# A gated attention and mixture-of-experts kernel: the routing between its halves rebuilt on other engines and types, bias loads issued from batch step eight on

## The reference

```python
x = x + tanh(g_xattn) * xattn(layernorm(x), ctx, ctx)      # retention with a decay mask
xf = layernorm(x).reshape(-1, 256)                          # 2048 tokens
scores = softmax(xf @ Wg.T)                                 # 8 experts
expert_weights, expert_indices = top_k(scores, 2)
expert_weights = expert_weights / expert_weights.sum(-1, keepdims=True)
gates = (one_hot(expert_indices, E) * expert_weights[..., None]).sum(axis=1)
h1 = xf @ (W1 + B1 A1).T + b1 ; h3 = xf @ (W3 + B3 A3).T + b3     # per expert, HID 512, rank 16
y_e = (silu(h1) * h3) @ (W2 + B2 A2).T + b2
out = x + tanh(g_ffn) * sum_e gates[e] * y_e
```

## Time and profile before

| | us |
|---|---|
| median of 3 runs | 347.4 (344.05 to 348.44) |
| profiled execution | 345.2 |
| its span, first to last instruction | 343.4 |
| busy in the span: TensorE / VectorE / ScalarE / GpSimd | 308.8 / 259.2 / 183.2 / 194.2 |
| mean granted TensorE clock | 0.968 |
| batch steps, from the start to the last top-eight search | 119.1 |
| routing, to the first matmul of the first tile | 23.2 |
| tiles, from there to the end | 201.0 |

### The profile page before, as it was taken

How to read it: one execution, slowest core, us unless ns; L and a number is a source line. 1 busy time by engine, 2 the same in 40 slices (tenths; PEclk the granted TensorE clock), 3 DMA queues, 4 the chain that set the end, 5 groups by cost and what they waited for, 6 DMA issues and landing times.

```text
span 343.4 us, 6837 instructions
## 1 busy us (share of the span) xinstructions
PE 308.8 (90%) x1766; PEld 234.3 (68%) x1766; DVE 259.2 (76%) x638; ACT 183.2 (53%) x387; POOL 194.2 (57%) x171
## 2 busy tenths in 40 slices
PE   8589989999997377999999999999999999999970
PEld 3468777778886324467777777777777777777750
DVE  2679797879996599278877788778877788777850
ACT  4646655666775611265565555655565555655540
POOL 1459886878988616514564556554564556454331
PEclk9899999899999769999999999999999999999997
DMA  7937799899878269403332233333331333234100
...
DMA packets 28098, 43.82 MB, mean 128 GB/s; under 512 B 6960, under 2 KB 15536, under 8 KB 27792
## 3 DMA queue, kind: packets, MB, share of 16 engines
...
...
## 4 chain that ended last, share of the span: by engine, by line
PE 63%; POOL 9%; DVE 8%; DMA 8%; issue 4%; ACT 4%; SPq 1%; POOLq 1%; ACTq 0%; DVEq 0%
PE bank L497 31%; PE bank L514 15%; POOL WL L700 5%; DMA xs<-x_in 5%; PE bank L505 5%; PE bank L487 2%; PE bank L345 2%; DMA WH<-lora_in 2%; DVE stage L783 2%; ACT WH L578 2%; PE bank L443 1%; PE bank L388 1%; PE bank L450 1%; DVE st L798 1%; PE bank L404 1%
## 5 line engine op out<-in xcount | busy, mean ns | idle before, releaser
L761 POOL DMA_INDIRECT out<-ys,sidx x39 | 61.9, 1586 | 85.6 <-DVE gsel L1010 61.8
L700 POOL TENSOR_TENSOR WL<-stage,WH 128x512 bf16<-128x512 f32 x48 | 60.4, 1279 | 18.1 <-ACT WH L578 17.8
L497 PE MATMUL bank<-WH,xh 128*128 x156 | 56.0, 440 | 0.6 <-ACT xh L658 0.6
L685 ACT ACTIVATE ys<-BB,gsel 128x256 f32 x39 | 19.8, 509 | 55.0 <-DMA out<-ys,sidx 52.9
L497 PE MATMUL bank<-WH,xl 128*128 x156 | 48.9, 394 | 0.0
L751 POOL DMA_INDIRECT xg<-xn_rows,gidx x39 | 38.8, 995 | 15.2 <-issue 12.4
L497 PE MATMUL bank<-WL,xb 128*128 x156 | 47.3, 385 | 0.0
L578 ACT ACTIVATE WH<-stage 128x512 fp32r<-128x512 f32 x48 | 29.6, 631 | 22.4 <-DVE stage L783 22.2
L1025 DVE TENSOR_TENSOR h<-bank,BB 128x512 f32<-128x512 f32 x39 | 27.0, 691 | 15.7 <-PE bank L497 15.6
L664 ACT ACTIVATE gh<-bank 128x512 fp32r<-128x512 f32 x39 | 23.4, 599 | 26.8 <-PE bank L505 26.8
L497 PEld LDWEIGHTS bank<-WH,xl 128*128 128x128 f32 x156 | 29.2, 188 | 7.7 <-DVE xl L1016 0.5
...
## 6 DMA issues: line engine op xcount, KB each, us to landing
...
```

Source lines behind the costliest of these rows:

```text
L497: last = nc.tensor.matmul(dst[:, :], lhs[p][:, c * P:(c + 1) * P], W[:, bass.ds(e * (UNITS * UC) + (2 * kind + c) * UC, HID)], start=(part ...
L700: nc.gpsimd.tensor_tensor(w_dst(WL, s, m), stage[(u * UNITS + m) % NSTAGE][:], w_dst(WH, s, m).bitcast(F32), ALU.subtract).then_inc(s_wl, 1)
L761: nc.gpsimd.indirect_dma_start(out=out_rows, out_offset=bass.IndirectOffsetOnAxis(ap=sidx[:, i:i + 1], axis=0), in_=ys[p][:], in_offset=No ...
```

## The change

The routing's tiles are bf16 and laid out with the 8 columns of a round innermost, so that each instruction's operands run with unit step; `AT` becomes `AT` (two buffers, two planes), `PP` and `IN2`. The scan runs over each partition's own `H` ahead of TensorE (`HS`), and TensorE's `trim` and `ones` products add up to the whole rank in one bank. GpSimd's multiplication goes to VectorE (`high`). The row number is no longer split in two sums: both parts are added by TensorE in the same columns of PSUM (two matmuls for each column of pairs, 16 a round instead of 8, whose weights are `BS[:, :, w]`), and which of the two experts it is is told by an indicator of 1 or 2 (`twice`). `gidx` is copied from PSUM at once and the gathers start on it (`s_rows`), ahead of `sidx`, `eid` and the selectors. The sums for the first 14 columns (`early_counts`) and constants (`constants`, `grids`) are made in steps 8 and 9. The wait for all stores now stands in `early_counts` and `grids`, ahead of the last top-eight search and of the last `first_two`. The search reads PSUM. The gates are multiplied and stored by ScalarE. `cst` is loaded in SP's turn 3. The bias loads wait for what last used the bytes that they overwrite; the buffers are laid out anew for it (that part of the diff, declarations only, is left out). Numbers of `keep_clock` change.

```diff
     for t in range(2, B):
         turn(t, t % 2)
+        if t == 3:
+            sp.dma_start(cst[:], consts).then_inc(s_cst, 16)
     turn(B, 0, more=False)
     turn(B + 1, 1, more=False)
-    sp.dma_start(cst[:], consts).then_inc(s_cst, 16)
-    sp.wait_ge(s_store, 32 * B)
-    sp.wait_ge(s_wl, E * UNITS)
-    sp.wait_ge(s_L, B)
+    sp.wait_ge(s_vproj, B)
+    sp.wait_ge(s_qrot, B)
+    sp.wait_ge(s_x2, B - 1)
     for e in range(E):
+        if e == 4:
+            sp.wait_ge(s_out, B)
+        if e == 6:
+            sp.wait_ge(s_unit, E * UNITS)
+        if e == 7:
+            sp.wait_ge(s_wl, (E - 1) * UNITS + 2)
         sp.dma_start(BB[:, e, :], biases[e:e + 1, :].to_broadcast([P, BCOL])).then_inc(s_bb, 16)
-        if e == 0:
-            sp.wait_ge(s_gates, 1)
-            sp.dma_start(xn2_d[:, D:D + K].rearrange("(j p) k -> p j k", p=P), gate[:]).then_inc(s_gates_d, 16)
...
         if three:
+            if not two:
+                keep_clock(10, WL, pK)
             pe.wait_ge(s_xn2, s - 1)
...
-            pos_wait(pe, s_L, s - 2)
+            pos_wait(pe, s_top, 2 * (s - 2))
...
-    Hf = H[:].rearrange("p e j -> p (e j)")
+    Hf, Cf = [t[:].rearrange("p e j -> p (e j)") for t in (H, HS)]
     pe.wait_ge(s_H, 1)
-    nc.tensor.matmul(pK[:, 0:P], tri[:], Hf, start=True, stop=True)
-    nc.tensor.matmul(pQ[:, 0:P], ones[:], Hf, start=True, stop=True).then_inc(s_rank, 1)
-    keep_clock(16, WL)
-    q = KJ // 4
-    for kj in range(KJ):
-        if kj % q == 0:
-            pe.wait_ge(s_bs, kj // q + 1)
-            pe.wait_ge(s_atj, kj // q + 1)
-            pe.wait_ge(s_atp, kj // q + 1)
-        last = nc.tensor.matmul(pV[:, 0:3 * NT_SLOTS], BS[kj // q % 2][:, kj % q, :],
-                                AT[:, kj].rearrange("p a i -> p (a i)"), start=(kj == 0), stop=(kj == KJ - 1))
-        if kj % q == q - 1:
-            last.then_inc(s_slots, 1)
-            keep_clock(4, WL)
-    keep_clock(22, WL)
+    nc.tensor.matmul(pO[:, 0:E], ones[:], HS[:, :, NJ - 1], start=True, stop=True).then_inc(s_total, 1)
+    nc.tensor.matmul(pK[:, 0:P], trim[:], Hf, start=True, stop=False)
+    nc.tensor.matmul(pK[:, 0:P], ones[:], Cf, start=False, stop=True).then_inc(s_rank, 1)
+    keep_clock(11, WL)
+    for c in range(4):
+        pe.wait_ge(s_bs, c + 1)
+        pe.wait_ge(s_hi, c + 1)
+        pe.wait_ge(s_pp, c + 1)
+        if c >= 2:
+            pe.wait_ge(s_twice, c - 1)
+        for w in range(KQ):
+            nc.tensor.matmul(pV[:, 0:2 * NT_SLOTS].rearrange("p (a i) -> p a i", a=2), BS[c % 2][:, :, w],
+                             AT[c % 2][:, :, :, w], start=(c == 0 and w == 0), stop=False)
+            last = nc.tensor.matmul(pV[:, 0:NT_SLOTS], BS[c % 2][:, :, w], PP[c % 2][:, :, w],
+                                    start=False, stop=(c == 3 and w == KQ - 1))
+        last.then_inc(s_slots, 1)
+    keep_clock(15, WL)
...
-    pe.wait_ge(s_routed, 1)
+    x_transposes(0, 0)
+    pe.wait_ge(s_eid, 1)
     read_expert(0, 0)
-    x_transposes(0, 0)
...
-        nc.scalar.activation(idxf[:, :, b * TPB:(b + 1) * TPB], I8[:, :, 0:K].rearrange("p t k -> p k t"), ACT.Copy
-                             ).then_inc(s_two, 1)
+        if b < B - 1:
+            nc.scalar.activation(idxf[:, :, b * TPB:(b + 1) * TPB], I8[:, :, 0:K].rearrange("p t k -> p k t"), ACT.Copy
+                                 ).then_inc(s_two, 1)
+    def grids():
+        act.wait_ge(s_cst, 16)
+        act.wait_ge(s_qT, 2 * B)
+        nc.scalar.activation(tiles_x[:], cst[:, C_TILE:C_TILE + NT_SLOTS].unsqueeze(2).to_broadcast([P, NT_SLOTS, KQ]),
+                             ACT.Copy).then_inc(s_grid, 1)
+        act.wait_ge(s_store, 32 * B)
+        nc.scalar.activation(slots_x[:], cst[:, C_IOTA:C_IOTA + P].unsqueeze(2).to_broadcast([P, P, KQ]), ACT.Copy
+                             ).then_inc(s_grid, 1)
...
         if two:
             hi(0, 1)
         if three:
+            if not two:
+                grids()
...
+    def planes(c):
         act.wait_ge(s_ind, c + 1)
-        nc.scalar.activation(AT[:, c * q:(c + 1) * q, 1, :], AT[:, c * q:(c + 1) * q, 2, :], ACT.Copy,
-                             scale=cst[:, C_P:C_P + 1]).then_inc(s_atp, 1)
+        if c >= 2:
+            act.wait_ge(s_slots, c - 1)
+            nc.scalar.activation(AT[c % 2][:, 1], IN2[c % 2][:], ACT.Copy, scale=2.0).then_inc(s_twice, 1)
+        nc.scalar.activation(PP[c % 2][:], AT[c % 2][:, 1] if c < 2 else IN2[c % 2][:], ACT.Copy, scale=cst[:, C_P:C_P + 1]
+                             ).then_inc(s_pp, 1)
+    planes(0)
+    act.wait_ge(s_w, 1)
+    for k, w in enumerate((wa, wb)):
+        nc.scalar.activation(gate[:, :, k], w[:], ACT.Copy, scale=tg[:, 1:2]).then_inc(s_gates, 1)
+    act.wait_ge(s_gates, K)
+    act.dma_start(xn2_d[:, D:D + K].rearrange("(j p) k -> p j k", p=P), gate[:]).then_inc(s_gates_d, 16)
+    for c in range(1, 4):
+        planes(c)
...
     act.wait_ge(s_routed, 1)
+    act.wait_ge(s_eid, 1)
+    x_parts(0, 0)
     act.wait_ge(s_bb, 16 * E)
-    x_parts(0, 0)
     tile_steps(act, tile)
...
-    pool.wait_ge(s_routed, 1)
     pool.wait_ge(s_gates_d, 16)
+    pool.wait_ge(s_rows, 1)
     for i in range(XBUF - 1):
         gather(i)
+    pool.wait_ge(s_routed, 1)
...
+    def constants():
+        dve.wait_ge(s_cst, 16)
+        dve.wait_ge(s_qT, 2 * B)
+        nc.vector.tensor_scalar(trim[:], cst[:, C_TRI:C_TRI + P], -1.0, None, ALU.add).then_inc(s_trim, 1)
+        for k in range(K):
+            nc.vector.tensor_scalar(hi_x[:, k * NJ:(k + 1) * NJ], cst[:, C_HI:C_HI + NJ], float(P), None, ALU.mult
+                                    ).then_inc(s_hix, 1)
+    def experts_of(j0, j1):
+        n = j1 - j0
+        nc.vector.tensor_tensor(OH[:, :, :, j0:j1],
+                                cst[:, C_E:C_E + E].unsqueeze(1).unsqueeze(3).to_broadcast([P, K, E, n]),
+                                idxf[:, :, j0:j1].unsqueeze(2).to_broadcast([P, K, E, n]), ALU.is_equal).then_inc(s_oh, 1)
+        dve.wait_ge(s_oh, 1 if j0 == 0 else 3)
+        nc.vector.tensor_tensor(H[:, :, j0:j1], OH[:, 0, :, j0:j1], OH[:, 1, :, j0:j1], ALU.add).then_inc(s_oh, 1)
+    def early_counts():
+        dve.wait_ge(s_two, 2 * (B - 1))
+        experts_of(0, JL)
+        dve.wait_ge(s_store, 32 * B)
+        nc.vector.memset(ones[:], 1.0)
+        nc.vector.memset(one8[:], 1.0)
...
-        def row_maxima():
+        def sorted_eight():
             dve.wait_ge(s_logit, b + 1)
-            nc.vector.tensor_copy(L8[:], pL[:, 0:TPB * E].rearrange("p (t e) -> p t e", t=TPB)).then_inc(s_L, 1)
-        def sorted_eight():
-            dve.wait_ge(s_L, b + 1)
             pos_wait(dve, s_two, 2 * b)
             for t in range(TPB):
-                last = nc.vector.max(M8[:, t, :], L8[:, t, :])
+                last = nc.vector.max(M8[:, t, :], pL[:, t * E:(t + 1) * E])
             last.then_inc(s_top, 1)
...
+        if two and not one:
+            constants()
         if two:
             dve.wait_ge(s_scores, s)
             pos_wait(dve, s_out, s - 1)
...
             if not two:
                 add(E - 1, 1, 4)
                 add(E - 1, 1, 5)
-            row_maxima()
+            if not two:
+                early_counts()
...
+    dve.wait_ge(s_top, 2 * B)
+    nc.vector.tensor_copy(idxf[:, :, JL:NJ], I8[:, :, 0:K].rearrange("p t k -> p k t")).then_inc(s_last, 1)
+    dve.wait_ge(s_last, 1)
+    experts_of(JL, NJ)
+    dve.wait_ge(s_oh, 4)
+    flat = lambda t: t[:].rearrange("p e j -> p (e j)")
+    nc.vector.tensor_tensor_scan(flat(HS), col(C_SEG, P), flat(H), 0.0, ALU.mult, ALU.add).then_inc(s_H, 1)
+    dve.wait_ge(s_two, 2 * B - 1)
+    nc.vector.tensor_tensor(dl[:], M2[:, :, 1], M2[:, :, 0], ALU.subtract).then_inc(s_dl, 1)
     dve.wait_ge(s_wl, E * UNITS)
+    dve.wait_ge(s_total, 1)
+    then(nc.vector.tensor_scalar(ti[:], pO[:, 0:E], float(P - 1), None, ALU.add))
+    then(nc.vector.tensor_scalar(ts[:], ti[:], 7, None, ALU.arith_shift_right))
+    then(nc.vector.tensor_copy(nt[:], ts[:]))
+    then(nc.vector.tensor_tensor_scan(tend[:], one8[:], nt[:], 0.0, ALU.mult, ALU.add))
+    then(nc.vector.tensor_tensor(base[:], tend[:], nt[:], ALU.subtract))
+    dve.wait_ge(s_rank, 1)
+    then(nc.vector.scalar_tensor_tensor(flat(Z), base[:].unsqueeze(2).to_broadcast([P, E, NJ]), float(P), pK[:, 0:P],
+                                        ALU.mult, ALU.add))
+    then(nc.vector.tensor_tensor(PK[:], OH[:], Z[:].unsqueeze(1).to_broadcast([P, K, E, NJ]), ALU.mult))
+    then(nc.vector.reduce_sum(pos[:], PK[:].rearrange("p k e j -> p k j e"), axis=AX))
+    then(nc.vector.tensor_copy(posi[:], pos[:].rearrange("p k j -> p (k j)")))
+    nc.vector.tensor_scalar(sli[:], posi[:], P - 1, None, ALU.bitwise_and)
+    then(nc.vector.tensor_scalar(tli[:], posi[:], 7, None, ALU.arith_shift_right))
+    nc.vector.tensor_copy(slb[:], sli[:])
+    then(nc.vector.tensor_copy(tlb[:], tli[:]))
+    dve.wait_ge(s_grid, 2)
```

(31 more changed lines are left out.)

135 lines of the change are left out of this document (39 added, 96 removed).

## The result

| kernel | median us | lowest to highest | runs |
|---|---|---|---|
| before | 347.75 | 344.05 to 348.44 | 4 |
| changed | 352.81 | 352.09 to 354.13 | 4 |

The ratio changed to before is 1.019 (95% interval 1.014 to 1.025). By the medians the change makes the kernel about 5 us slower. Forecast were 344.5 and at most 349.5: the prediction was wrong, on the sign and outside its range. The profiled execution took 352.09 us, its span is 350.2. Some executions fall in a state that is about 1% longer; the medians count them and the ratios don't, so the two differ a little in the last experiments.

The account below looks back on a forecast made before the run. Bound by the VectorE routing chain before the first tile's matmul, with tiles running gapless on TensorE: gained 6.0, lost 5 to delayed stores and 0.3 to `cst`, so 0.7 off 345.2 gives 344.5 us; range 338.5 to 349.5.

Parts of the forecast that it names:

- S: Time at which VectorE may start the last top-eight search; forecast 118.2 us if the stores are undisturbed.
- the 0.3 taken for `cst`: Moving the `cst` load into step three, where DMA is busy, costs between nothing and 0.9 us; 0.3 taken.
- I take 5 us: Delay of the last two stores, and so of the last search, by early bias loads sharing the DMA engines.
- the 5.7 from which my own text says that the sign turns: Store delay in us from which the change was forecast to make the kernel slower instead of faster.
- the first rival: Stores wait out the whole bias backlog, search starts at 127, first matmul 2.8 us later, 348.3 us; chance 17%.
- The second rival, whole turns: DMA engines alternate queues by whole turns, so stores land only 2.4 us late: 341.9 us; whole turns or less 30%.
- Top-eight to tile numbers: Routing chain from the last search's start to the tile numbers (`tlb`'s end), forecast at 5.7 us.
- The four rounds: One-hots and matmul sums of four column groups, forecast to end 7.1 + 0.5 us after the tile numbers, against 9.4 before.
- 0.5 for the stride: Extra time in the four rounds for matmul weights read at a 16-byte stride; bounds nothing and 2 us.
- To the first matmul: From summed groups to gather 0.5 us (0.2 conversion, 0.3 start), then 4.3 to the first tile's matmul.
- the third rival: Sparser routing leaves TensorE at half clock, closing dummy matmuls outlast the gather, first tile slow: 3 to 4 us, 348; 8%.
- biases cost nothing on this path: Bias loads begun ten us earlier finish before the first gather, so their own time adds nothing there.

Follow-up runs that it names:

- the kernel with two loads early: Changed kernel with bias loads 0 and 1 issued in step eight, the other six held behind the 16 stores: 345.49 us, ratio 0.998.
- The probe: Changed kernel plus 48 unused 78-column matmuls ahead of the rounds, weights and moving operand contiguous or strided: 0.063 us each with contiguous moving operand, 0.14 strided.

## Why the prediction was wrong

By its own marks: it had S at 118.2 + 5 = 123.2, t0 (`tlb`'s end) at 128.9, the gather at 137.0, the first tile matmul at 141.3. Measured were 127.59, 132.99, 143.50 and 148.34. Of the 7.0 us between, 4.4 are in S, -0.3 in the chain to t0, 2.95 behind t0. With 0.8 more in the tiles and the 0.3 taken for `cst`, which did not show up in any step before the eighth, that is the whole distance from 344.5 to the profiled 352.09.

**The step that failed: "I take 5 us" for the stores.** Measured: 9.0 more from issue to landing (12.0 for 3.0), and 0.4 from an issue at 115.52 instead of 115.15. The mechanism was right, and so was its price: one for one by packets, 32 packets of 0.2 us, 6.4; measured, the passage took 8.0 (118.6 to 126.6) instead of 1.7, 6.3 more. What the number lacked is in the two steps around it. I cut 6.4 to 5 for the stream's start and its pauses, but the share of the DMA engines was 1.02 in 115 to 120 and 1.04 in 120 to 126: there were none. And I gave the start of the stores no time: their first packet came 3.5 us after the issue, against 0.8 before, while bias packets filled the DMA engines. That is 2.7. The 9.0 lie above the 5.7 from which my own text says that the sign turns, and so does the 6.4 alone: the rows' own sum was past the turn, and yet only 17% stood on that side. The landing of 12 us is the first rival's mark, but it came by another path. The stores did not wait until the biases were through; they passed one for one after a late start, and both ran out nearly together, the stores' packets at 126.6 and the biases' near 128. That the number was the rival's is chance.

**The second rival, whole turns** (the page "DMA: Bandwidth & Descriptors" of the Trainium skill, section "Queues, rings and completion order"), falls. 449 packets of one queue went beside 443 of the other, and shrinking the bias packets from 5 KB to 1 KB shortened the store's landing by 4 us. By the prediction's sum for whole turns the store would have landed 2.4 us late; it was 9.0 late. Whole turns should also show as stretches of one queue and then of the other, and every slice of 0.4 us shows both alike. The measurement decides. (That rival's figure for no delay, 339.2, leaves out the 0.3 for `cst`; with it, it is 339.5.)

**A term put at nothing.** The undisturbed S was 118.2, the landing of the last store. But the same stretch now holds the early one-hots and their sum. They took 1.17 and 1.16 us beside GpSimd's subtractions and ended at 119.50, so S could not be earlier than that; with the biases late it was 119.97 and 119.70. The wait for the stores hides this in the changed kernel. With the sums' stride and GpSimd's late start below, it is why the kernel with two loads early shows 2.3 of the 6.0 us forecast as gained.

**Top-eight to tile numbers** held: S + 5.4, forecast 5.7. The prediction's own terms add up to 5.5, not 5.7.

**The four rounds**: bf16 instructions took 0.32 and 0.68, as forecast (0.32, 0.69). The term "0.5 for the stride" was about right for the weights, which cost 0.4 in four rounds, and left out the moving operand. The sums ended at t0 + 9.35, not 7.6. The probe shows that a strided moving operand costs 1.8 ns a column, 1.8 us a round of 8 pairs against 1.0 forecast. I bounded only the weights and overlooked that the moving operand had become strided as well. The moving planes had been contiguous in the kernel before (0.59 for eight of 117), and the new layout, which gives VectorE its unit steps, took that from TensorE. With my upper bound for a stride (2 us) the sums would have ended at t0 + 9.1, near what was measured; I chose 0.5 against it since the trace showed loads that overlap.

**To the first matmul**: the gather started 1.16 after the sums' end, not 0.5, of which 0.44 belongs to GpSimd's long wait. From gather to first matmul it took 4.84, not 4.3, since the 15 dummies ran at half clock until 146.1 (5.32 us in all) and ended at 147.48, while the rows had landed near 146.5.

**TensorE's clock**, the third rival, was partly real. The granted clock fell to 0.5 at 139.4, amid the sums. Its price was the 0.5 to 0.8 us above, not the 3 to 4 forecast: the first tile had full clock, and the strided matmuls take as long at either clock (a pair in 0.22 us at 137 and at 141).

**The gates** were harmless in the changed kernel, with the biases long through, and cost about 2 us as soon as the biases were moved back. My arithmetic "biases cost nothing on this path" held only for the order that cost 9 us elsewhere.
